# Every engine's order in a graph-attention kernel written out call by call, with the last quarter picked in three pieces

## The chip, the cores and the metric

One core of a Trainium2 chip. The metric is the device time of one execution in microseconds (us), of which 255.73 us is the median of three runs of the kernel before (254.72 to 261.86).

## What is computed

The inputs are x, 4096 x 128, and a dense 4096 x 4096 adjacency matrix in fp32 (64 MB), with few ones. The reference, cut to what matters:

```python
h = jnp.maximum(_layernorm(x, axis=-1), 0.0)
Wh = h @ W
e = leaky_relu((Wh @ a[:d_out])[:, None] + (Wh @ a[d_out:])[None, :], 0.2)
mask = (adj > 0) | jnp.eye(N, dtype=bool)
x = x + softmax(where(mask, e, -9e15), axis=1) @ Wh
h = jnp.maximum(_layernorm(x, axis=-1), 0.0)
x = x + where(adj < 1.0, exp(-(1.0 / adj - 1.0) ** 2 / 0.5), 0.0) @ (h @ W1 + B1)
```

Where every entry of the matrix is 0 or 1, the weights of the last line are all zero, so the kernel computes the attention layer alone and verifies, over the whole matrix, that each entry is 0 or 1. A general path (not run with these inputs) is taken if one is not.

## The kernel before

The matrix is read in 32 **chunks** of 2 MB, two to a **step** (16 steps), eight to a **quarter** of the rows (four quarters, `s` = 0 to 3). SyncE loads chunk i into slot i % 6 of a ring of six, once chunk i - 6 has been used by everyone. For each chunk these pieces of work are issued:

- `check(i)` verifies that its entries are 0 or 1: on ScalarE two passes (L866, L869), or on VectorE one pass (L1035). `DVE_CHECKED` lists the chunks that VectorE takes, all others are ScalarE's.
- `pack(i)` on TensorE turns eight rows' bits and the column number into one word per column in PSUM (L560, L573), and VectorE's `scan(step)` takes the largest words of each segment out of PSUM (L1065) when both chunks of the step are packed.
- `clean_diagonal(i)` and `column(i)` on VectorE, `turn_hub` and `turn_columns` on TensorE, and `hub`/`hub_group` treat the diagonal and the first 128 nodes (the hubs) apart.

A **piece** is a group of steps whose non-zeros are picked together. For piece n the chain is: `pick(n)` (VectorE, rounds of 8 largest), `place(n)` (TensorE), then two branches. The lane branch: `decode(n)` (VectorE) writes `index`. The shared branch: `pick_shared(n)` (VectorE, L1108 to L1131), `place_shared(n)` (TensorE, L646), `decode_shared(n)` (VectorE, L1145 to L1168) writes `shared_index`. GpSimd then issues one indirect DMA for each slot of the group (L478), which gathers rows of a node table in DRAM. When a **group** g has landed, `weigh(g)` (VectorE; L1222 to L1233 for a lane group, to L1239 or L1251 for a shared one) makes weights, and `scatter(g)` (TensorE, L682) adds the group to the accumulators in PSUM. Before, the pieces are the steps 0-3, 4-7, 8-11, 12-14 and 15; they make 11 groups (0 to 10) of 76 indirect DMAs. Groups share a ring of four, so group g is gathered only after group g - 4 has been scattered.

The accumulators of a quarter are begun by `add_columns(s)` (TensorE, L670), get `add_self(s)` (L677, after ScalarE's `scale_self(s)`, L889) and the scatters, and are emptied by `epilogue(s)` (VectorE, L1313 and L1319, eight tiles), after which SyncE stores the quarter. `add_columns(s + 1)` waits for `epilogue(s)`, since both use the same banks. The last quarter ends with `weigh(10)`, `scatter_last` and `last_epilogue` in three parts. `judge()` (VectorE) collects all verdicts of the checks, and `count_bad` (TensorE) must stand before `scatter_last` in TensorE's queue.

Each engine runs its own queue in program order. Before, that order came from a loop over the chunks with tables that say at which chunk a call stands, for instance:

```python
DVE_CHECKED = [0, 1, 4, 2, 5, 7, 10, 12, 14, 17, 19, 21, 31]
SCAN_AT = {2 * n + 2: n for n in range(STEPS - 1)}
PICK_AT = {8: 0, 16: 1, 24: 2, 30: 3}
WEIGH_AT = {13: 0, 15: 1, 17: 2, 20: 3, 22: 4, 25: 5, 28: 6}
EPILOGUE_AT = {19: 0, 27: 1}
```

## Time and profile before

| | |
|---|---|
| Median of 3 runs | 255.73 us (254.72 to 261.86) |
| The profiled execution | 253.61 us, of which the span from first to last instruction is 251.8 us |
| TensorE busy | 170.7 us (68%) |
| VectorE busy | 186.3 us (74%) |
| ScalarE busy | 188.1 us (75%) |
| GpSimd busy | 120.9 us (48%) |
| Mean granted clock of TensorE | 0.846 |
| Moved by DMA | 76.96 MB |

In the rows below, PE is TensorE, DVE VectorE, ACT ScalarE, POOL GpSimd and SP SyncE; PEld is TensorE's weight load. All times are us from the start of the span. In a row of the timeline the numbers are the start and the length, then come engine, line, operation, output<-inputs, count, and in brackets how long the engine sat idle before it and what ended that wait ("remote": no recorded end of an instruction fits the semaphore's change). An end of a matrix multiplication is modelled, so the start of what waited for it is the firmer number.

### The profile page before, as it was taken

Reading aid. Unit: us, or ns where it says so; the run is one execution under the profiler, and the core shown is the slowest. Engines: PE = TensorE matmul, PEld = TensorE weight load, DVE = VectorE, ACT = ScalarE, POOL = GpSimd, SP = SyncE. Lnnn points to the kernel's source line nnn. Section 1 sums busy time; section 2 is a strip of 40 time slices with the busy share of each in tenths; the row PEclk is TensorE's granted clock in tenths of the full one; section 3 lists DMA queues with packets and bytes.
Section 4 is the critical chain, followed back from the end, with each engine's and each line's share of the span. In section 5 each row is a group of like instructions: output and inputs, shape, how many; then the busy total and the mean of one; then the engine's idle time right before and its main releaser. Section 6 shows DMA issues by size and latency. Waiting matters only on the chain. (4 is left out here: it accounts for less than half of the span.)

```text
span 251.8 us, 3251 instructions
## 1 busy us (share of the span) xinstructions
PE 170.7 (68%) x970; PEld 118.5 (47%) x970; DVE 186.3 (74%) x563; ACT 188.1 (75%) x201; POOL 120.9 (48%) x131
## 2 busy tenths in 40 slices
PE   0296797595149849794999787557494929557390
PEld 0295553253135525563576554434353626356390
DVE  7967949989988799999599993865317581067963
ACT  0899876977993089899983999999999999900000
POOL 0395040000007798987689898137760027713810
PEclk9999999979557986999599999797887776965778
DMA  5999999999999999999999999999994001120002
GB/s 160 389 410 411 407 410 415 422 411 408 409 409 405 390 394 395 403 394 395 392 393 401 398 391 397 390 408 389 384 392 187 0 5 40 26 85 0 9 10 90
DMA packets 22389, 76.96 MB, mean 306 GB/s; under 512 B 2643, under 2 KB 3255, under 8 KB 22368
## 3 DMA queue, kind: packets, MB, share of 16 engines
q1 hardware_dynamic: 18912, 71.31, 72.5%
q0 software_dynamic: 3040, 5.34, 6.3%
q8 instruction: 9, 0.15, 0.2%
q10 hardware_dynamic: 416, 0.07, 0.2%
q14 instruction: 12, 0.10, 0.1%
HBM read 74.52 MB, written 4.28 MB: 313 GB/s over the span
## 5 line engine op out<-in xcount | busy, mean ns | idle before, releaser
L478 POOL DMA_INDIRECT gathered_rows<-node_table,index x48 | 68.1, 1418 | 73.2 <-issue 45.2
L573 PE MATMUL bank<-adj_ring,pack_w 128*128 128x512 bf16 (+3 forms) x262 | 73.9, 411 | 5.4 <-DVE clean L1051 2.9
L866 ACT ACTIVATE trash_a<-adj_ring,below_one 128x4096 fp8e4<-128x4096 f32 x19 | 70.4, 3705 | 4.3 <-DMA adj_ring<-in_adj 3.3
L869 ACT ACTIVATE trash_a<-adj_ring 128x4096 fp8e4<-128x4096 f32 x19 | 68.7, 3618 | 0.6
L1035 DVE SCALAR_TENSOR_TENSOR trash_v<-adj_ring 128x4096 fp8e4<-128x4096 f32 x13 | 57.3, 4411 | 0.1
L478 POOL DMA_INDIRECT gathered_rows<-node_table,shared_index x28 | 37.7, 1345 | 17.6 <-DVE shared_index L1156 9.4
L573 PEld LDWEIGHTS bank<-adj_ring,pack_w 128*128 128x128 bf16 x262 | 27.3, 107 | 37.7 <-issue 17.6
L682 PE MATMUL bank<-gathered_rows,spread 128*128 128x129 f32 x176 | 27.3, 321 | 8.9 <-DVE spread L1233 8.6
L1065 DVE MAX8 cand<-bank 128x8 f32<-128x120 f32 (+24 forms) x82 | 23.3, 349 | 11.5 <-PE bank L573 8.0
L682 PEld LDWEIGHTS bank<-gathered_rows,spread 128*128 128x128 f32 x176 | 25.9, 233 | 10.2 <-issue 9.9
L895 ACT ACTIVATE bad_terms<-bank 1x48 f32<-1x48 f32 x1 | 0.2, 200 | 22.7 <-PE bank L699 22.7
L878 ACT ACTIVATE r_rows<-bank 128x512 f32<-128x512 f32 x8 | 4.6, 590 | 16.0 <-remote 11.0
L610 PE MATMUL bank<-whe,hub_w 128*128 128x129 f32 x64 | 10.5, 319 | 7.7 <-DVE hub_w L1272 7.3
L560 PE MATMUL bank<-codes,code_w 128*128 128x512 bf16 x32 | 14.2, 445 | 1.8 <-issue 1.8
L1313 DVE RECIPROCAL rden<-bank 128x3 f32<-128x3 f32 (+1 forms) x12 | 2.0, 168 | 16.6 <-remote 16.5
L610 PEld LDWEIGHTS bank<-whe,hub_w 128*128 128x128 f32 x64 | 9.5, 227 | 9.3 <-DVE hub_w L1272 8.8
L835 ACT ACTIVATE spread<-x_sb,shift,rstd 128x128 f32<-128x128 f32 x32 | 13.3, 502 | 0.0
L670 PE MATMUL bank<-hub_whe,col_w 128*128 128x129 f32 x48 | 7.8, 328 | 7.3 <-DVE x_sb L1319 7.3
L629 PE MATMUL bank<-slots,own_lane 128*32 128x8 f32 (+1 forms) x40 | 2.4, 192 | 14.8 <-issue 13.1
L510 PE MATMUL bank<-w_sb,gathered_rows 128*128 128x130 f32 x64 | 10.5, 315 | 1.3 <-ACT whe L849 1.2
L498 PE MATMUL bank<-ident,spread 128*128 128x128 f32 x32 | 6.5, 338 | 6.8 <-ACT spread L835 6.8
L670 PEld LDWEIGHTS bank<-hub_whe,col_w 128*128 128x128 f32 x48 | 7.2, 238 | 7.9 <-issue 7.9
(165 smaller groups left out, 269.9 us busy)
## 6 DMA issues: line engine op xcount, KB each, us to landing
adj_ring<-in_adj SPq DMA_DIRECT2D x32, 2048.0 KB, 18.1
node_table<-whe POOLq DMA_DIRECT2D x4, 532.0 KB, 10.9
x_sb<-in_x SPq DMA_DIRECT2D x8, 256.0 KB, 6.0
out<-x_sb SPq DMA_DIRECT2D x3, 512.0 KB
gathered_rows<-node_table,index POOLq DMA_INDIRECT x48
gathered_rows<-node_table,shared_index POOLq DMA_INDIRECT x28
out<-x_sb SPq DMA_DIRECT2D x2, 192.0 KB
out<-x_sb SPq DMA_DIRECT2D x1, 128.0 KB
```

The costliest lines, as they stand in the source:

```text
L478: pool.indirect_dma_start(out=rows[:, g % RING_GROUPS * GE + t, :], out_offset=None, in_=table, in_offset=bass.IndirectOffsetOnAxis(ap=row ...
L510: last = nc.tensor.matmul(bank[6 + half][:, b * (D + 2):(b + 1) * (D + 2)], hT[:, nb * P:(nb + 1) * P], w0_sb[:, :], start=(b == 0), stop= ...
L560: nc.tensor.matmul(to[:, :], code_w[:, 2 * c + half, :], codes[:, :], start=True, stop=False, skip_group_check=True)
L573: last = nc.tensor.matmul(to[:, lo:hi], pack_w[:, k, :], ring_hi[:, i % AR, row_at + lo:row_at + hi], start=False, stop=(k == KB - 1), ski ...
L610: last = nc.tensor.matmul(bank[7][:, 0:E1], hub_w[:, m % 2, b, :], whe[:, 4 * HUB_ORDER[m] + b, ONE:ONE + E1], start=(m + b == 0), stop=(m ...
L670: last = nc.tensor.matmul(acc_of(t), weights[:, t, :], hub_whe[:, ONE:ONE + E1], start=(t % 3 == 0), stop=True, skip_group_check=True)
L682: return nc.tensor.matmul(acc_of(t), spread[:, g % 2, t * KB:(t + 1) * KB, :], rows[:, g % RING_GROUPS * GE + turn, ONE:ONE + E1], start=F ...
L835: last = nc.scalar.activation(hn_block(b), x_sb[:, b, :], ACT.Identity, bias=shift[:, b:b + 1], scale=rstd[:, b:b + 1])
L866: nc.scalar.activation(trash_a[:, :], ring[:, i % AR, :], ACT.Sign, bias=below_one[:, :], scale=-1.0, accum_out=signs[:, n:n + 1], saturat ...
L869: nc.scalar.activation(trash_a[:, :], ring[:, i % AR, :], ACT.Abs, accum_out=sizes[:, n:n + 1], saturate=False).then_inc(checked_a, 1)
L1035: nc.vector.scalar_tensor_tensor(trash_v[:, :], ring[:, i % AR, :], 1.0, ring[:, i % AR, :], ALU.is_ge, ALU.not_equal, accum_out=bad_v[:, ...
L1065: last = nc.vector.max(cand[:, at * 8:(at + 1) * 8], word_bank(step, half)[:, lo:hi])
```

## The change

The tables and the loops over the chunks are gone: each engine's calls stand written out in a list. What differs in it:

- Pieces: steps 12 to 14 and 15 become 12 and 13, 14, and 15. Pieces 4 (step 14) and 5 (step 15) have no lane group. There are 12 groups (0 to 11) and 80 indirect DMAs.
- VectorE checks chunks 1, 2, 0, 4, 7, 10, 14, 12, 16, 18, 21, 24 (12 chunks instead of 13, and no chunk after 24); ScalarE checks 20 instead of 19, the last of them in the order 30, 28, 31, 29.
- `shared_index` and `shared_on` have three buffers instead of two; a few waits are added so that the new order is sound (`self_added`, `words_done`).

```diff
 PIECES = [((0, 1, 2, 3), 32, 16, 32), ((4, 5, 6, 7), 24, 16, 16), ((8, 9, 10, 11), 24, 8, 32),
-          ((12, 13, 14), 16, 8, 16), ((15,), 8, 0, 16)]
+          ((12, 13), 16, 8, 16), ((14,), 8, 0, 16), ((15,), 8, 0, 16)]
-DVE_CHECKED = [0, 1, 4, 2, 5, 7, 10, 12, 14, 17, 19, 21, 31]
-ACT_CHECKED = [i for i in range(CHUNKS) if i not in DVE_CHECKED]
+DVE_CHECKED = [1, 2, 0, 4, 7, 10, 14, 12, 16, 18, 21, 24]
+ACT_CHECKED = [3, 5, 6, 8, 9, 11, 13, 15, 17, 19, 20, 22, 23, 25, 26, 27, 30, 28, 31, 29]
-PICK_AT = {8: 0, 16: 1, 24: 2, 30: 3}
-WEIGH_AT = {13: 0, 15: 1, 17: 2, 20: 3, 22: 4, 25: 5, 28: 6}
-        shared_index = sb("shared_index", [P, 2, KB], i32)
+        shared_index = sb("shared_index", [P, 3, KB], i32)
...
@@ the tail of TensorE's list @@
-            add_columns(SG - 1)
+            turn_columns(27)
+            pack(28)
+            add_columns(2)
+            place(3)
+            pack(29)
+            add_self(2)
+            place_shared(3)
+            pack(30)
+            scatter(6)
             place(4)
+            pack(31)
             place_shared(4)
-            add_self(SG - 1)
+            scatter(7)
+            place(5)
+            add_columns(3)
+            place_shared(5)
             scatter(8)
             scatter(9)
+            add_self(3)
+            scatter(10)
             count_bad()
             scatter_last()
@@ of ScalarE's @@
+            row_weights(3, 1)
+            check(25)
+            check(26)
+            check(27)
+            check(30)
+            check(28)
+            check(31)
+            check(29)
             raise_flag()
@@ of VectorE's @@
+            pick(2)
+            clean_diagonal(24)
+            weigh(4)
+            decode(2)
+            pick_shared(2)
+            clean_diagonal(25)
+            decode_shared(2)
+            weigh(5)
+            check(24)
+            column(26)
+            scan(12)
+            scan(13)
+            epilogue(1)
+            column(27)
+            pick(3)
+            pick_shared(3)
+            decode(3)
+            weigh(6)
+            decode_shared(3)
+            scan(14)
+            pick(4)
+            weigh(7)
+            pick_shared(4)
+            scan(15)
+            decode_shared(4)
+            pick(5)
             epilogue(2)
-            scan(STEPS - 1)
-            pick(4)
-            pick_shared(4)
-            decode_shared(4)
-            check(CHUNKS - 1)
+            pick_shared(5)
             weigh(8)
+            decode_shared(5)
             weigh(9)
+            weigh(10)
             judge()
-            weigh(10)
+            weigh(11)
             last_epilogue()
```

Three places show what moves. **VectorE, around the scan of step 15.** Before (L1168 ends `decode_shared(3)`, L1313 and L1319 are `epilogue(2)`, L1065 is `scan(15)`, then `pick(4)`):

```order
L1168 TENSOR_TENSOR shared_on<-stats,std 128x128
L1313 RECIPROCAL rden<-bank 128x3
L1319 SCALAR_TENSOR_TENSOR x_sb<-bank,rden,x_sb 128x128 x3
L1313 RECIPROCAL rden<-bank 128x3
L1319 SCALAR_TENSOR_TENSOR x_sb<-bank,rden,x_sb 128x128 x3
L1313 RECIPROCAL rden<-bank 128x2
L1319 SCALAR_TENSOR_TENSOR x_sb<-bank,rden,x_sb 128x128 x2
L1065 MAX cand<-bank 128x8 x4
L1078 TENSOR_REDUCE full<-cand 128x1
```

Of the change (L1205 ends `pick_shared(4)`, L1137 is `scan(15)`, L1219 to L1242 is `decode_shared(4)`, L1150 begins `pick(5)`):

```order
L1205 TENSOR_SCALAR full<-shared_slots 32x1
L1137 MAX cand<-bank 128x8 x4
L1219 CAST shared_i<-bank 128x4
L1220 TENSOR_SCALAR shared_empty<-bank 128x4
L1222 TENSOR_SCALAR shared_column<-shared_i 128x4
L1224 TENSOR_SCALAR shared_lane<-shared_i 128x4
L1230 TENSOR_TENSOR shared_index<-shared_column,shared_empty 128x4
L1232 TENSOR_TENSOR stats<-shared_i,shared_mask 128x32
L1236 TENSOR_TENSOR std<-shared_lane,lane_number 128x16
L1240 TENSOR_SCALAR stats<-stats 128x32
L1242 TENSOR_TENSOR shared_on<-stats,std 128x128
L1150 TENSOR_REDUCE full<-cand 128x1
```

The scan of step 15 no longer stands behind `epilogue(2)`; the epilogue now follows the pick of step 15.

**VectorE, behind the last `decode_shared`.** Before (L1168 ends `decode_shared(4)`, L1035 is `check(31)`, L1222 begins `weigh(8)`):

```order
L1166 TENSOR_SCALAR stats<-stats 128x32
L1168 TENSOR_TENSOR shared_on<-stats,std 128x128
L1035 SCALAR_TENSOR_TENSOR trash_v,verdicts<-adj_ring 128x4096
L1222 TENSOR_TENSOR edge_w<-r_slots,gathered_rows 128x64
L1225 TENSOR_TENSOR edge_w<-edge_w,gathered_rows 128x64
```

Of the change (L1242 ends `decode_shared(5)`, L1296 begins `weigh(9)`):

```order
L1240 TENSOR_SCALAR stats<-stats 128x32
L1242 TENSOR_TENSOR shared_on<-stats,std 128x128
L1296 TENSOR_TENSOR same<-r_pair,gathered_rows 128x128
L1299 TENSOR_TENSOR same<-same,gathered_rows 128x128
L1302 TENSOR_TENSOR same<-same,shared_on 128x128
```

No check is left on VectorE behind the last index list.

**TensorE, from `add_columns(2)` to the last `pack`.** Before (L670 `add_columns(2)`, L573 x8 `pack(29)`, L682 `scatter(6)`, L629 and L636 `place(3)`, L646 `place_shared(3)`, L560 and L573 x4 `pack(30)`, L677 `add_self(2)`, L682 `scatter(7)`, L573 x8 `pack(31)`):

```order
L573 MATMUL bank<-adj_ring,pack_w 128x512 x8
L682 MATMUL bank<-gathered_rows,spread 128x129 x8
L629 MATMUL bank<-slots,own_lane 32x8 x4
L636 MATMUL bank<-turn_of_p,placed 128x8
L646 MATMUL bank<-half_of_tq,stats 128x4
L560 MATMUL bank<-codes,code_w 128x512
L573 MATMUL bank<-adj_ring,pack_w 128x512 x4
L560 MATMUL bank<-codes,code_w 128x512
L573 MATMUL bank<-adj_ring,pack_w 128x512 x4
L677 MATMUL bank<-whe,ident 128x129 x8
L682 MATMUL bank<-gathered_rows,spread 128x129 x8
L573 MATMUL bank<-adj_ring,pack_w 128x512 x8
```

Of the change (L612 and L619 `place(3)`, L555 x8 `pack(29)`, L660 `add_self(2)`, L629 `place_shared(3)`, L542 and L555 x4 `pack(30)`, L666 `scatter(6)`, L612 `place(4)`, L555 x8 `pack(31)`):

```order
L612 MATMUL bank<-slots,own_lane 32x8 x4
L619 MATMUL bank<-turn_of_p,placed 128x8
L555 MATMUL bank<-adj_ring,pack_w 128x512 x8
L660 MATMUL bank<-whe,ident 128x129 x8
L629 MATMUL bank<-half_of_tq,stats 128x4
L542 MATMUL bank<-codes,code_w 128x512
L555 MATMUL bank<-adj_ring,pack_w 128x512 x4
L542 MATMUL bank<-codes,code_w 128x512
L555 MATMUL bank<-adj_ring,pack_w 128x512 x4
L666 MATMUL bank<-gathered_rows,spread 128x129 x8
L612 MATMUL bank<-slots,own_lane 32x8 x4
L555 MATMUL bank<-adj_ring,pack_w 128x512 x8
```

`place(3)` comes before `pack(29)`, and `scatter(7)` comes behind `pack(31)`.

## Rows read from the trace of the kernel before

**Rows 1.** The page: span, and granted clock and DMA in 40 slices.

```profile
span 251.8 us, 3251 instructions
...
PEclk9999999979557986999599999797887776965778
DMA  5999999999999999999999999999994001120002
```

**Rows 2.** Timeline of SP: the three last chunk loads, and the first store.

```profile
164.67 15.92 SPq L347 DMA_DIRECT2D adj_ring<-in_adj  x3
180.64 42.63 SPq L352 DMA_DIRECT2D out<-x_sb  x3
```

**Rows 3.** Stretches: start:end, length, DVE busy (count), granted clock, DMA share, GB/s.

```profile
153.20:158.00 4.80, 0.00 (x0) 1.00 1.03 395
158.00:171.10 13.10, 10.82 (x49) 0.86 1.03 400
171.10:192.70 21.60, 8.04 (x29) 0.82 0.92 348
192.70:208.60 15.90, 11.84 (x48) 0.71 0.10 38
208.60:220.10 11.50, 0.02 (x1) 0.86 0.16 33
220.10:223.00 2.90, 2.69 (x11) 0.85 0.05 4
```

**Rows 4.** Timeline of DVE, last quarter.

```profile
158.03 0.22 DVE L1222 TENSOR_TENSOR edge_w<-r_slots,gathered_rows 128x64 f32<-128x64 f32 x1 [4.83 <-issue]
...
189.99 0.18 DVE L1313 RECIPROCAL rden<-bank 128x3 f32<-128x3 f32 x1 [4.99 <-remote]
...
220.11 0.18 DVE L1313 RECIPROCAL rden<-bank 128x3 f32<-128x3 f32 x1 [11.49 <-remote]
...
223.01 1.42 DVE L1065 MAX8 cand<-bank 128x8 f32<-128x272 f32 x4
...
229.67 0.16 DVE L1156 TENSOR_TENSOR shared_index<-shared_column,shared_empty 128x4 int32<-128x4 int32 x1
...
230.40 4.42 DVE L1035 SCALAR_TENSOR_TENSOR trash_v<-adj_ring 128x4096 fp8e4<-128x4096 f32 x1
...
242.13 0.29 DVE L1222 TENSOR_TENSOR same<-r_pair,gathered_rows 128x128 f32<-128x128 f32 x1 [2.17 <-DMA gathered_rows<-node_table,shared_index]
```

**Rows 5.** Timeline of PE, from `pack(29)` to `add_columns(3)`.

```profile
196.49 2.81 PE L573 MATMUL bank<-adj_ring,pack_w 128*128 128x512 bf16 x8
...
206.82 0.56 PE L646 MATMUL bank<-half_of_tq,stats 32*128 32x4 f32 x2 [4.13 <-DVE stats L1126]
...
213.51 1.95 PE L682 MATMUL bank<-gathered_rows,spread 128*128 128x129 f32 x16
215.30 1.97 PE L573 MATMUL bank<-adj_ring,pack_w 128*128 128x512 bf16 x8
223.05 3.78 PE L670 MATMUL bank<-hub_whe,col_w 128*128 128x129 f32 x16 [5.79 <-DVE x_sb L1319]
```

**Rows 6.** Timeline of POOL: an undisturbed issue, and the last group's first and last.

```profile
220.23 1.00 POOL L478 DMA_INDIRECT gathered_rows<-node_table,shared_index  x1 [0.30 <-issue]
230.61 5.08 POOL L478 DMA_INDIRECT gathered_rows<-node_table,shared_index  x1 [9.38 <-DVE shared_index L1156]
...
239.31 1.15 POOL L478 DMA_INDIRECT gathered_rows<-node_table,shared_index  x1 [0.30 <-issue]
```

**Rows 7.** Timeline of ACT: its two longest waits, and its last check's second pass.

```profile
87.12 0.60 ACT L878 ACTIVATE r_rows<-bank 128x512 f32<-128x512 f32 x1 [9.46 <-remote]
...
136.34 0.60 ACT L878 ACTIVATE r_rows<-bank 128x512 f32<-128x512 f32 x1 [5.01 <-PE bank L601]
...
213.41 3.71 ACT L866 ACTIVATE trash_a<-adj_ring,below_one 128x4096 fp8e4<-128x4096 f32 x1
...
217.24 3.62 ACT L869 ACTIVATE trash_a<-adj_ring 128x4096 fp8e4<-128x4096 f32 x1
```

More of the change, by code:

```diff
@@ L476, in _ @@
                     at = (g - FIRST_GROUP[n]) * GE + t
-                    row_of = shared_index[:, n % 2, t:t + 1] if IS_SHARED[g] else index[:, n % 3, at:at + 1]
+                    row_of = shared_index[:, n % 3, t:t + 1] if IS_SHARED[g] else index[:, n % 3, at:at + 1]
                     pool.indirect_dma_start(
@@ L760, in _ @@
-            add_columns(SG - 1)
+            pack(0)
+            quad_scores(0)
+            turn_hub(0)
+            pack(1)
+            quad_scores(1)
+            pack(2)
+            pack(3)
+            turn_hub(2)
+            pack(4)
+            hub_group(0)
+            pack(5)
+            hub_group(1)
+            turn_hub(4)
+            pack(6)
+            turn_columns(4)
+            pack(7)
+            hub_group(2)
+            hub_group(3)
+            turn_columns(5)
+            pack(8)
@@ new lines, in _ @@
+            turn_hub(6)
+            place(0)
+            hub_group(4)
+            row_scores(1, 0)
+            pack(9)
+            pack(10)
+            hub_group(5)
+            pack(11)
+            hub_group(6)
+            row_scores(1, 1)
+            place_shared(0)
+            pack(12)
+            pack(13)
+            hub_group(7)
+            add_columns(0)
+            pack(14)
+            add_self(0)
+            turn_columns(14)
+            pack(15)
+            spread_hub()
@@ new lines, in _ @@
+            turn_columns(15)
+            scatter(0)
+            place(1)
+            pack(16)
+            pack(17)
+            place_shared(1)
+            pack(18)
+            scatter(1)
+            pack(19)
+            scatter(2)
+            row_scores(2, 0)
+            row_scores(2, 1)
+            pack(20)
+            add_columns(1)
+            pack(21)
+            turn_columns(20)
+            pack(22)
+            turn_columns(21)
+            pack(23)
+            row_scores(3, 0)
@@ new lines, in _ @@
+            add_self(1)
+            place(2)
+            scatter(3)
+            pack(24)
+            place_shared(2)
+            pack(25)
+            row_scores(3, 1)
+            scatter(4)
+            pack(26)
+            turn_columns(26)
+            pack(27)
+            scatter(5)
+            turn_columns(27)
[7 more added lines that the diff above has]
+            scatter(6)
@@ new lines, in _ @@
+            quad_weights()
+            keep_hub(0)
+            check(3)
+            keep_hub(2)
+            pair_weights()
+            check(5)
+            keep_hub(4)
+            check(6)
+            keep_hub(6)
+            check(8)
+            check(9)
+            row_weights(1, 0)
+            check(11)
+            row_weights(1, 1)
+            scale_self(0)
+            keep_hub_rows()
+            check(13)
+            check(15)
+            check(17)
+            scale_self(1)
@@ L948, in _ @@
+            check(19)
+            row_weights(2, 0)
+            scale_self(2)
+            row_weights(2, 1)
+            check(20)
+            check(22)
+            row_weights(3, 0)
+            check(23)
+            scale_self(3)
+            row_weights(3, 1)
[6 more added lines that the diff above has]
+            check(29)
             raise_flag()
@@ L1073, in pick @@
                     dve.wait_ge(merged, n)
-                    dve.wait_ge(placed_set, n)
+                    dve.wait_ge(placed_set, sum(map(bool, LANE_GROUPS[:n])))
                     dve.wait_ge(full_seen, n)
@@ L1446, in _ @@
-            epilogue(2)
-            scan(STEPS - 1)
-            pick(4)
-            pick_shared(4)
-            decode_shared(4)
-            check(CHUNKS - 1)
+            check(1)
+            quad_masks()
+            check(2)
+            score_terms()
+            check(0)
+            own_and_hub_weights()
+            check(4)
+            scan(0)
+            clear_diagonal(4)
+            hub(0)
+            clean_diagonal(5)
+            scan(1)
+            hub(1)
+            hub(2)
@@ new lines, in _ @@
+            scan(2)
+            hub(3)
+            column(4)
+            clean_diagonal(8)
+            scan(3)
+            hub(4)
+            pick(0)
+            hub(5)
+            decode(0)
+            column(5)
+            clean_diagonal(9)
+            check(7)
+            hub(6)
+            scan(4)
+            hub(7)
+            pick_shared(0)
+            check(10)
+            scan(5)
+            decode_shared(0)
+            weigh(0)
+            check(14)
+            scan(6)
@@ new lines, in _ @@
+            check(12)
+            column(14)
+            scan(7)
+            pick(1)
+            column(15)
+            clean_diagonal(16)
+            weigh(1)
+            clean_diagonal(17)
+            decode(1)
+            pick_shared(1)
+            check(16)
+            weigh(2)
+            decode_shared(1)
+            scan(8)
+            check(18)
+            epilogue(0)
+            scan(9)
+            check(21)
+            column(20)
+            scan(10)
+            column(21)
@@ new lines, in _ @@
+            weigh(3)
+            scan(11)
+            pick(2)
[17 more added lines that the diff above has]
+            decode_shared(3)
```

265 lines of the change are left out of this document (94 added, 171 removed).

## The prediction

> **What bounds the kernel now.** I read the page's slices first. DMA stands at 9 tenths or more from the second slice to the thirtieth and is nearly empty after that [rows 1]. The 32 chunks stream at 395 to 400 GB/s with a DMA share of 1.03, and in the stretch to 192.70 the share is still 0.92; then it is 0.10 [rows 3]. The last load is issued near 180 us [rows 2]. So up to about 190 us the kernel is as fast as its loads, and a change of order can only spoil that part. Behind it stand 62 us (190 to 251.8) in which no chunk arrives: the tail is what the change can shorten.
>
> Next I read who waits in the tail. VectorE does 11.84 us of work in 192.7 to 208.6, then 0.02 us in the 11.5 us up to 220.1 [rows 3]. That hole of 11.49 us is the wait of `epilogue(2)` for `scatter(7)` [rows 4]. Only behind it, at 223.01, comes `scan(15)`, although chunk 31 had landed some 30 us before. TensorE shows the same from its side: it waits 4.13 us with `place_shared(3)` for VectorE and starts `pack(30)` behind that, near 207; `pack(31)` starts at 215.30 [rows 5]. The tail is a sequence of hand-overs between two engines, both mostly idle.
>
> From `scan(15)` to the end the times of before are: 223.01 to the last `shared_index` at 229.67, 6.66 us; to GpSimd's first issue at 230.61, 0.94; to the end of its fourth issue (239.31 + 1.15), 9.85; to the landing at 242.13, 1.67; to the end of the span, 9.67 [rows 4, 6]. Together 28.8 us. One of the four issues takes 5.08 us where an undisturbed one takes 1.00, and it lies exactly beside VectorE's `check(31)` of 4.42 us from 230.40 [rows 4, 6].
>
> **The sum.** I follow the new order from the end of `decode_shared(2)`, 171.10 before.
>
> *Head start.* Before, VectorE stood 4.83 us in front of `weigh(4)` [rows 4], since that call stood ahead of `scan(11)`; all of the stretch from 153.2 to 158.0 is empty [rows 3]. Now `weigh(4)` stands behind `pick(2)`. I take 5 us: `decode_shared(2)` ends at 166. The bounds are 0 (the chunks or ScalarE's `row_weights` hold it anyway) and 7.
>
> *To the end of `epilogue(1)`.* VectorE's work in the stretch that ended with it was 8.04 us [rows 3]. The change adds `check(24)`, 4.42, and puts `scan(13)` ahead of it, 1.42 by the row of `scan(15)` [rows 4]. 166 + 8.04 + 4.42 + 1.42 = 179.9, where it was 192.7. The three loads that were due by then are not late by this: `check(24)` ends near 173.
>
> *To `scan(15)`.* VectorE has 11.84 us less `scan(13)` plus `pick(4)` and `pick_shared(4)` (1.8), about 12. TensorE has more: `add_columns(2)` 3.78, then `place(3)`, `pack(29)`, `add_self(2)`, `place_shared(3)`, `pack(30)`, `scatter(6)`, `place(4)`, `pack(31)`. With 1.95 for eight 129-column fp32 multiplications, 1.97 for a `pack` (2.46 with the two more of an even chunk) and 0.56 for each of the three small ones [rows 5] this is 15.8 us. At half the clock, with 3.78 for the 129-column ones and a `pack` doubled, it is 25.8; the granted clock in these stretches was 0.71 to 0.86 [rows 3]. I take 19, and 2 for the turns in which TensorE waits for `pick_shared(3)` and `pick_shared(4)`. `scan(15)` starts at 201 instead of 223. It cannot come before about 194, by the landing of chunk 31.
>
> *From `scan(15)` to the end.* The scan 1.42; `decode_shared(4)` and `pick(5)` 1.8 (their instructions lie in the 6.66 of before); `epilogue(2)` 2.69; `add_columns(3)` 3.78, ahead of `place_shared(5)` in TensorE's queue; `place_shared(5)` 0.56; 0.4 to the index: 10.7. Then 0.94, four issues of 1.00 + 0.30 = 5.2, landing 1.67, and 9.67: 28.2 us [rows 3 to 6]. So what `check(31)` gives back (9.85 - 5.2 = 4.65) is spent on having `epilogue(2)` and `add_columns(3)` inside this stretch, which is now as long as before.
>
> The indirect DMAs: group 8 waits for the lane index of piece 3, now near 185 where it was 205; twelve issues of 1.3 us are over near 201, so groups 8 and 9 are off the path, as are the four added issues of 5.2 us. The smaller edits (third buffers, added waits) cost nothing: what they wait for lies behind on the same queue or is over.
>
> *Late signals.* `scatter(7)` ends at 213.51 + 1.95 = 215.46 by its row, yet `epilogue(2)`, which waits for nothing else, begins at 220.11: 4.65 us late [rows 4, 5]. The wait of 4.99 us at 189.99 is of this kind. I do not know the cause; both lie beside GpSimd's long runs of issues. The new order has such a run too. I charge it once, 4.6. The bounds are 0 and twice.
>
> The Trainium skill, page "TensorE: Matmul & The Clock Gate", section on the cost of a per-tile semaphore tail, gives some 26 ns for each increment that a matrix multiplication makes. By it no signal would be late, and the sum would be 4.6 us shorter; the rows above say otherwise, and the rows decide.
>
> Span: 201 + 28.2 + 4.6 = 233.8, where it was 251.8. Outside the span the profiled execution had 1.8 us (253.61 - 251.8): 235.6. That execution lay 2.1 under the median of the runs; I add 1.4 for it and predict **237 us**.
>
> **The rivals.**
>
> *ScalarE becomes the bound.* Its last check ended at 217.24 + 3.62 = 220.9, and nobody waited for it. Now it has one check more, 3.71 + 3.62 + some 0.3 = 7.6, and `judge()`, `count_bad` and the last scatters wait for it. For: 228.5 if no idle time is saved, then 0.5 for the verdicts and the same 9.67: span 238.7, time 240.5 to 242. Against: it idled 9.46 and 5.01 us in the middle [rows 7], and its order is rewritten there. With ten of these saved it ends near 218 and the last landing (201 + 4.6 + 18.5 = 224) is later.
>
> *Every hand-over is late* (the other side). The new order has more of them in the tail: `place(3)`, `place_shared(3)`, `scan(14)`, `place(4)`, `scan(15)`, `place_shared(4)`, `epilogue(2)`, `place(5)`, `place_shared(5)`. If eight of nine pay 4.65 as `epilogue(2)` did, it is 37 us: 229.2 + 37 + 1.8 = 268, slower. It decides from 20.8 us on (within 2%: from 16 to 26), that is 2.6 us at each of eight. Against: before, `place_shared(3)` to `decode_shared(3)` and `scan(14)` were prompt, and a lateness that all signals share at one time is paid once when they follow each other.
>
> *A hole in the loads.* `check(24)` moves from ScalarE to VectorE and stands behind `weigh(5)`, which waits for a gather; load 30 waits for it, and `check(7)` and `check(12)` come later than before. A load must be issued before the one ahead has landed, about 180 for load 30. I expect 173. If the lists slip by 7 us and more, each further us is paid in full: 5 us give 242.
>
> *It does not do what it says.* `scan(15)` comes early but the last `shared_index` stays where it is, since `add_columns(3)`, `scatter(7)` and both packs now crowd TensorE at half the clock: 25.8 instead of 19 and as much again behind the scan, +14 us, 251.
>
> **How the numbers follow.** The forecast has 0.68, ScalarE's bound 0.12, a hole in the loads 0.07, no gain 0.06, late hand-overs 0.07 (half of it slower, half of it the same). With the head start at its bounds (+5, -2), TensorE's sum (+7, -3) and the late signals (+4.6, -4.6) not all at one end, the forecast's own range is 230 to 246. To 248 it takes in ScalarE's bound and most holes. A measurement of this kernel tells about 2% from no change (250.6 to 260.8). Faster by more than 2%: 0.87; within: 0.09; slower: 0.04.
>
> **What would show it.** Right: VectorE's `scan(15)` (L1137, the last) near 201 and its hole of 11.5 us gone; GpSimd's last four issues near 1.0 us each, beginning near 213 to 217; `pack(30)` before `pack(31)` with no wait of 4 us; DMA as full as before up to 190. ScalarE's last pass should end at 216 to 222. Wrong would be: DMA below 9 tenths before slice 29, the last pass of ScalarE after 226, or several waits of 3 us and more on VectorE behind TensorE's signals between 185 and 215. The head start is wrong if `epilogue(1)` ends later than 185.

## The result, and the profile after

The changed kernel took **236.5 us** (median of four, 234.53 to 238.15), the kernel before in the same comparison 256.97 (254.72 to 261.86): ratio 0.9205, 95% interval 0.906 to 0.935. The forecast was 237. The profiled execution has a span of 233.5 us at a mean granted clock of 0.880 (forecast 233.8; before 251.8). Some executions of either kernel are a few per cent longer at a lower clock; medians and their ranges take in all executions, ratios and their intervals only the others, so a ratio is not always the quotient of two medians.

From the page of the changed kernel, busy times and the slices:

```profile
PE 164.8 (71%) x982; PEld 117.6 (50%) x996; DVE 186.6 (80%) x591; ACT 195.4 (84%) x205; POOL 129.4 (55%) x135
...
DVE  7984999999199999499992799988999078177972
ACT  0899978999859996999796669999399999999930
...
DMA  5999999999999999999999999999999992003002
```

The loads fill the same stretch as before [rows 1]. VectorE is busy as long as before (186.6 us against 186.3), ScalarE 7.3 us longer and GpSimd 8.5 longer. What went is idle time in the tail.

VectorE's timeline of the changed kernel: start, duration, engine and line, operation, shapes, and in brackets the idle time before it and its releaser. "remote" means that no recorded end of an instruction fits the change that released it:

```profile
165.09 0.42 DVE L1242 TENSOR_TENSOR shared_on<-stats,std 128x256 f32<-128x256 f32 x1
...
178.32 0.16 DVE L1388 RECIPROCAL rden<-bank 128x2 f32<-128x2 f32 x1
...
188.06 0.18 DVE L1182 TENSOR_TENSOR mv<-bank,iota 32x32 f32<-32x32 f32 x1 [7.16 <-remote]
...
200.65 0.18 DVE L1182 TENSOR_TENSOR mv<-bank,iota 32x32 f32<-32x32 f32 x1 [3.05 <-remote]
...
205.69 1.43 DVE L1137 MAX8 cand<-bank 128x8 f32<-128x272 f32 x4 [3.78 <-remote]
...
215.88 0.16 DVE L1230 TENSOR_TENSOR shared_index<-shared_column,shared_empty 128x4 int32<-128x4 int32 x1
...
223.39 0.18 DVE L1411 SCALAR_TENSOR_TENSOR excess<-sizes,signs 128x20 f32<-128x20 f32 x1 [1.23 <-ACT trash_a L909]
```

`decode_shared(2)` ends at 165.5 (171.10 before), `epilogue(1)` near 179.1 (192.7), `scan(15)` starts at 205.69 (223.01), the last `shared_index` is written at 215.9 (229.67 before) [rows 4]. From `scan(15)` to the end of the span are 27.8 us. The hole of 11.49 us in front of `epilogue(2)` is gone, but three waits with "remote" have come: `pick_shared(3)`, `pick_shared(4)`, `scan(15)`. TensorE's timeline of the same kernel:

```profile
181.57 0.39 PE L619 MATMUL bank<-turn_of_p,placed 128*128 128x8 f32 x2
...
183.63 2.14 PE L660 MATMUL bank<-whe,ident 128*128 128x129 f32 x16
190.10 0.58 PE L629 MATMUL bank<-half_of_tq,stats 32*128 32x4 f32 x2 [4.33 <-DVE bits_i L1271]
...
196.87 1.98 PE L555 MATMUL bank<-adj_ring,pack_w 128*128 128x512 bf16 x8
```

`pack(31)` ended at 198.85, and VectorE, idle and waiting for nothing else, began `scan(15)` at 205.69: 6.8 us late. `place(3)` (its last rows are L619) ended near 182 and `pick_shared(3)` began at 188.06, 6.1 late. The ends of multiplications are modelled, but here the queue itself shows that `place(3)` was over: TensorE had gone on to `pack(29)` and `add_self(2)` (L660), done at 185.8. Then it stood 4.33 us in front of `place_shared(3)`, for VectorE's late `pick_shared(3)`. The prediction called this late signals.

GpSimd and ScalarE of the changed kernel:

```profile
168.08 5.24 POOL L460 DMA_INDIRECT gathered_rows<-node_table,index  x1 [0.30 <-issue]
...
190.45 1.00 POOL L460 DMA_INDIRECT gathered_rows<-node_table,index  x1 [4.11 <-DVE index L1262]
...
216.81 0.99 POOL L460 DMA_INDIRECT gathered_rows<-node_table,shared_index  x1 [3.45 <-DVE shared_index L1230]
...
220.74 1.07 POOL L460 DMA_INDIRECT gathered_rows<-node_table,shared_index  x1 [0.30 <-issue]
```

```profile
219.65 3.62 ACT L909 ACTIVATE trash_a<-adj_ring 128x4096 fp8e4<-128x4096 f32 x1
```

The last four issues take 5.0 us (9.85 before [rows 6]); the stretched one now stands beside `check(24)`, at 168.08. ScalarE's last pass ends at 223.3, and `judge` waits 1.23 us for it. So at the end two bounds lie side by side, the last gather and ScalarE.

### The profile page after: what moved, and what is told of

Read it like the earlier page. It is cut to its first block, busy times and chain, and to the rows that moved or that the text cites. A ratio compares the mean times of both kernels' runs of the same rounds, so it can differ in the third digit from the quotient of the medians.

```text
span 233.5 us, 3347 instructions
## 1 busy us (share of the span) xinstructions
PE 164.8 (71%) x982; PEld 117.6 (50%) x996; DVE 186.6 (80%) x591; ACT 195.4 (84%) x205; POOL 129.4 (55%) x135
## 4 chain that ended last, share of the span: by engine, by line
ACT 31%; issue 26%; POOL 13%; DVE 10%; DMA 7%; PE 7%; SPq 2%; another core or an unknown queue 2%; POOLq 0%; DVEq 0%; ACTq 0%
ACT trash_a L906 16%; ACT trash_a L909 13%; POOL gathered_rows L460 13%; DMA adj_ring<-in_adj 7%; DVE trash_v L1106 6%; PE bank L555 3%; ACT whe L946 2%; PE bank L666 2%; SPq L337 2%; PE bank L637 1%; DVE x_sb L1394 1%; DVE spread L1313 1%; PE bank L505 0%; PE bank L584 0%
## 5 line engine op out<-in xcount | busy, mean ns | idle before, releaser
L460 POOL DMA_INDIRECT gathered_rows<-node_table,index x48 | 75.5, 1573 | 49.5 <-issue 42.9
L906 ACT ACTIVATE trash_a<-adj_ring,below_one 128x4096 fp8e4<-128x4096 f32 x20 | 74.1, 3707 | 4.7 <-DMA adj_ring<-in_adj 3.8
L555 PE MATMUL bank<-adj_ring,pack_w 128*128 128x512 bf16 (+3 forms) x255 | 69.6, 402 | 8.9 <-DMA adj_ring<-in_adj 5.1
L909 ACT ACTIVATE trash_a<-adj_ring 128x4096 fp8e4<-128x4096 f32 x20 | 72.3, 3617 | 0.6
L1106 DVE SCALAR_TENSOR_TENSOR trash_v<-adj_ring 128x4096 fp8e4<-128x4096 f32 x12 | 53.0, 4414 | 1.0 <-DMA adj_ring<-in_adj 1.0
L460 POOL DMA_INDIRECT gathered_rows<-node_table,shared_index x32 | 37.6, 1175 | 14.7 <-issue 11.2
L555 PEld LDWEIGHTS bank<-adj_ring,pack_w 128*128 128x128 bf16 x262 | 26.3, 105 | 35.6 <-issue 9.0
L666 PE MATMUL bank<-gathered_rows,spread 128*128 128x129 f32 x192 | 30.4, 324 | 7.0 <-DVE spread L1313 4.6
L666 PEld LDWEIGHTS bank<-gathered_rows,spread 128*128 128x128 f32 x192 | 28.7, 235 | 8.4 <-issue 8.0
L1137 DVE MAX8 cand<-bank 128x8 f32<-128x120 f32 (+24 forms) x82 | 23.2, 351 | 3.8 <-remote 3.8
L946 ACT ACTIVATE whe<-whe,w_self 128x129 f32<-128x129 f32 x32 | 9.8, 389 | 1.9 <-PE bank L593 1.9
L542 PE MATMUL bank<-codes,code_w 128*128 128x512 bf16 x25 | 10.0, 399 | 1.9 <-DMA adj_ring<-in_adj 1.9
L492 PE MATMUL bank<-w_sb,gathered_rows 128*128 128x130 f32 x64 | 10.2, 311 | 1.4 <-ACT whe L889 1.3
L492 PEld LDWEIGHTS bank<-w_sb,gathered_rows 128*128 128x128 f32 x64 | 9.2, 221 | 2.6 <-ACT gathered_rows L881 2.4
L1394 DVE SCALAR_TENSOR_TENSOR x_sb<-bank,rden,x_sb 128x128 f32<-128x128 f32 x32 | 9.4, 345 | 0.4
```

Of the source, the lines that this page charges most:

```text
L460: pool.indirect_dma_start(out=rows[:, g % RING_GROUPS * GE + t, :], out_offset=None, in_=table, in_offset=bass.IndirectOffsetOnAxis(ap=row ...
L492: last = nc.tensor.matmul(bank[6 + half][:, b * (D + 2):(b + 1) * (D + 2)], hT[:, nb * P:(nb + 1) * P], w0_sb[:, :], start=(b == 0), stop= ...
L555: last = nc.tensor.matmul(to[:, lo:hi], pack_w[:, k, :], ring_hi[:, i % AR, row_at + lo:row_at + hi], start=False, stop=(k == KB - 1), ski ...
L666: return nc.tensor.matmul(acc_of(t), spread[:, g % 2, t * KB:(t + 1) * KB, :], rows[:, g % RING_GROUPS * GE + turn, ONE:ONE + E1], start=F ...
L906: nc.scalar.activation(trash_a[:, :], ring[:, i % AR, :], ACT.Sign, bias=below_one[:, :], scale=-1.0, accum_out=signs[:, n:n + 1], saturat ...
L909: nc.scalar.activation(trash_a[:, :], ring[:, i % AR, :], ACT.Abs, accum_out=sizes[:, n:n + 1], saturate=False).then_inc(checked_a, 1)
```

## The experiments

Each study ran on one chip, with the kernel before beside it; the four studies ran on four different chips. Which chip it was turned out to go with a larger difference than most edits made.

### First study: parts of the change

The kernel before took 235.2 us here (233.67 to 237.95, 14 runs), not 256. What these four show holds for a chip on which the kernel before takes that time; the second study has the kernel before at 258. The expectations were all written against 256 and the changed kernel's 236.5, and the changed kernel itself was not run on this chip, so their times cannot be held against these runs as they stand.

**a_head_only**: the old tail behind the new head.

```
-          ((12, 13), 16, 8, 16), ((14,), 8, 0, 16), ((15,), 8, 0, 16)]
+          ((12, 13, 14), 16, 8, 16), ((15,), 8, 0, 16)]
 weigh(5)
-check(24)
-column(26)
-scan(12)
-scan(13)
...
+scan(12)
+column(26)
+epilogue(1)
+scan(13)
...
```

> The new order up to decode_shared(2) and weigh(5) on VectorE (and to the same place on the other engines), behind it the old order, with the old pieces (steps 12 to 14, 15), 11 groups, check(24) on ScalarE and check(31) on VectorE. It prices the head start by itself. Theory of the prediction: decode_shared(2) ends near 166 instead of 171, and all that follows moves by the same 5 us: 251 to 252 against 256.5 of before, scan(15) near 218. Rival, the head start is eaten later (by the loads, which end near 190 in both, or by signals that come late): 255 to 257, scan(15) near 223. Rival, most of the gain is already here: 242 or less.

Measured: 238.6 us, 1.018 of before (1.012 to 1.024). None of the three held: 238.6 lies under the 242 of the last one, but that meant a large gain, and here the kernel is slower than before. The head alone brings nothing on this chip. VectorE waits 8.8 us at 178.2 for ScalarE's `row_weights(3, 1)`, which stands behind `check(24)` and `check(25)`. Its row:

```profile
178.16 0.81 DVE L1357 TENSOR_SCALAR col_w<-r_rows,hub_whe 128x1024 f32<-128x1024 f32 x1 [8.76 <-ACT r_rows L915]
```

**b_check31_act**: one edit in the kernel before.

```
-DVE_CHECKED = [0, 1, 4, 2, 5, 7, 10, 12, 14, 17, 19, 21, 31]
+DVE_CHECKED = [0, 1, 4, 2, 5, 7, 10, 12, 14, 17, 19, 21]
 decode_shared(4)
-check(CHUNKS - 1)
```

> The kernel before with one edit: the pass over chunk 31 is taken from VectorE (behind decode_shared(4)) and given to ScalarE as its last one. Theory of the prediction: GpSimd's four last issues take 5.2 us instead of 9.85, and nobody waits for ScalarE (last pass ends near 228.5, judge comes after it): 4.65 us less, 252. Rival, the issues are slow beside whatever VectorE does: same as before within 1 us. Rival, the late end of ScalarE holds judge and all that stands behind it: 255 or more.

Measured: 237.8 us, 1.015 (1.007 to 1.023): slightly slower; the last rival, ScalarE's late end holds `judge`, is what the trace shows. Up to `decode_shared(4)` it is the program of before on VectorE and GpSimd. VectorE's timeline:

```profile
178.32 0.18 DVE L1313 RECIPROCAL rden<-bank 128x3 f32<-128x3 f32 x1 [0.76 <-PE bank L682]
...
205.04 1.41 DVE L1065 MAX8 cand<-bank 128x8 f32<-128x272 f32 x4
...
209.75 0.16 DVE L1156 TENSOR_TENSOR shared_index<-shared_column,shared_empty 128x4 int32<-128x4 int32 x1
...
223.97 0.18 DVE L1335 SCALAR_TENSOR_TENSOR excess<-sizes,signs 128x20 f32<-128x20 f32 x1 [8.68 <-ACT trash_a L869]
```

`epilogue(1)` starts at 178.3 and not at 189.99, `scan(15)` at 205.0 and not at 223.01 [rows 4], with the same calls in the same order. No wait of VectorE has "remote" in the four traces of this chip. And the last issue ended at 216.2, but `judge` waited 8.7 us for ScalarE's pass over chunk 31: the gathers gained, and ScalarE took the gain and more.

**a_check31_dve**: the same pass, in the changed kernel, back on VectorE.

```
-DVE_CHECKED = [..., 18, 21, 24]
+DVE_CHECKED = [..., 18, 21, 24, 31]
 decode_shared(5)
+check(31)
```

> The changed kernel with the pass over chunk 31 given back to VectorE, behind decode_shared(5); ScalarE has one pass less and ends near 216. Theory 1, the path of the changed kernel runs through group 11's four gathers: one issue is stretched from 1.0 to some 5 us, so 4 to 5 us more, 240.5 to 241.5. Theory 2, ScalarE (last pass ends 223.4, judge waits 1.2 us for it) is as much a bound as the gathers: the same 4 to 5 us more, since the gathers landed at 222.9. Rival, ScalarE alone is the bound at the end: the same time or up to 1 us less.

Measured: 231.3 us, 0.983 (0.978 to 0.989). With ScalarE relieved (its last pass ended at 212.8) the time is low although one issue is stretched. That is nearest to the rival, but it does not settle it, for want of the changed kernel beside it. VectorE's, TensorE's and GpSimd's rows:

```profile
196.08 1.40 DVE L1136 MAX8 cand<-bank 128x8 f32<-128x272 f32 x4
...
206.43 0.16 DVE L1229 TENSOR_TENSOR shared_index<-shared_column,shared_empty 128x4 int32<-128x4 int32 x1
```

```profile
193.40 1.97 PE L555 MATMUL bank<-adj_ring,pack_w 128*128 128x512 bf16 x8 [1.65 <-DMA adj_ring<-in_adj]
```

```profile
207.46 5.21 POOL L460 DMA_INDIRECT gathered_rows<-node_table,shared_index  x1 [0.30 <-issue]
212.97 1.09 POOL L460 DMA_INDIRECT gathered_rows<-node_table,shared_index  x1 [0.30 <-issue]
```

The new order brings `scan(15)` to 196.1 where the old one had 205.0 on the same chip, 9 us, and here `pack(31)` waits for nothing but chunk 31. But the last index comes only 3.3 us earlier (206.4 against 209.8), and the first issue that uses it begins at 212.97, 6.4 us behind it. The stretched issue, still one of the added group 10, makes 4.2 of these; the rest is GpSimd's queue being behind with the twelve gathers of groups 8 and 9 and with group 10.

**a_pieces**: the third piece undone.

```
-          ((12, 13), 16, 8, 16), ((14,), 8, 0, 16), ((15,), 8, 0, 16)]
+          ((12, 13, 14), 16, 8, 16), ((15,), 8, 0, 16)]
 column(27)
+scan(14)
 pick(3)
...
```

> The changed kernel with the old pieces: steps 12 to 14 picked together, then 15, 11 groups, in a new order by hand (scan(14) ahead of pick(3); place(4) and add_columns(3) behind scatter(7)). It prices the third piece. Theory A, the third piece is worth what it costs or more, since group 8's gathers begin before step 14 is scanned: here group 8's first gather comes 3 to 5 us later than 190.45, and the time is 238 to 242. Theory B, the piece is worth nothing, since groups 8 and 9 are off the path and what is saved is work (one pick, one pick_shared, one decode_shared, four gathers, 10 us of GpSimd and VectorE in all): 233 to 237, scan(15) before 203.

Measured: 233.7 us, 0.994 (0.990 to 0.998). Theory B in its numbers: without the piece `scan(15)` starts at 196.9, and the last issue ends at 212.8. What holds the end is ScalarE, so the time does not tell what the third piece is worth:

```profile
220.33 0.18 DVE L1408 SCALAR_TENSOR_TENSOR excess<-sizes,signs 128x20 f32<-128x20 f32 x1 [8.70 <-ACT trash_a L906]
```

### Second study: both kernels again

> The kernel before, unedited, for its trace in this study, since the first four runs stood against 235.2 us and not against 256. Theory C, what cost the 20 us in the profiled execution of before is not in the program: TensorE's signals reach VectorE promptly here (no wait of 3 us and more behind a multiplication that had ended, save the 7 us in front of epilogue(2), where scatter(7) itself is late), index(3) near 192 instead of 205, scan(15) near 205 instead of 223, and the time 234 to 236. Rival, the loads or an engine's own work were slower in the first profile: then the same instructions take longer there, or the DMA share is lower, and this trace shows it.

> The changed kernel, unedited, against the kernel before in this study. Theory C: without late signals only what the program itself gives is left. ScalarE's last pass ended at 223.4 with the late signals and has no idle time that they made (but 4.2 us at 169.5), so the time is 231 to 235, 0 to 2% faster than before, and VectorE's hole in front of pick_shared(3) is 1 to 2 us instead of 7. Rival, the change is worth 18 to 20 us here too: 215 to 218.

On this chip the kernel before took 258.4 us (253.45 to 260.12, 7 runs; b_same 253.3 and 264.5), the changed one 239.3: 0.941 (0.936 to 0.946). So neither the times of Theory C nor its rival held here: this is a chip on which the 20 us are there again. The trace of b_same repeats the first profile, within 0.1 us at both places. VectorE in b_same:

```profile
189.94 0.18 DVE L1313 RECIPROCAL rden<-bank 128x3 f32<-128x3 f32 x1 [4.30 <-remote]
...
220.04 0.18 DVE L1313 RECIPROCAL rden<-bank 128x3 f32<-128x3 f32 x1 [11.52 <-remote]
```

In three of the four studies, and in the first comparison, the median of the kernel before was 256.6 to 260.4 us; in one it was 235.2. It goes with the chip, though each chip was used once, so that something else about the hour is not excluded. What differs in the traces is the waits behind TensorE.

The changed kernel had on this chip four such waits; the fourth, 8.4 us in front of `epilogue(2)`, is behind its longer time, since the last `shared_index` follows it:

```profile
187.29 0.18 DVE L1182 TENSOR_TENSOR mv<-bank,iota 32x32 f32<-32x32 f32 x1 [6.99 <-remote]
...
212.52 0.18 DVE L1388 RECIPROCAL rden<-bank 128x3 f32<-128x3 f32 x1 [8.36 <-remote]
```

**f_check28_dve**: the pass over chunk 28 put into the first of these holes.

```
 pick(3)
+check(28)
...
-check(28)   (ScalarE)
```

> The changed kernel with the pass over chunk 28 moved from ScalarE to VectorE, behind pick(3), where VectorE waited 7.2 us in the profile after. If ScalarE (last pass ends 223.4) is a bound, it now ends 7.6 us earlier and the time falls by 1 to 5 us, to 229 to 233. If VectorE's chain to scan(15) is the bound, the 4.4 us of the pass come on top where no late signal covers them: 235 to 239.

Measured: 238.3 us, 0.934 (0.919 to 0.949), against 0.941 for the changed kernel: 1 us, not told apart. It is the second case of the two expected. ScalarE was idle for 13 us at the end, so it was not the bound on this chip; VectorE still waited 4.4 us in front of `scan(15)` and 4.2 in front of `epilogue(2)`, both with "remote".

### Third and fourth study: why the signals are late

The kernel before took 260.4 (253.83 to 270.62) in the third and 256.6 (255.2 to 268.85) in the fourth. In these three kernels `pick_shared(3)`, `scan(15)` and `epilogue(2)` stand where they stood; only groups 7, 8 and 9 fetch nothing, or other rows, so their results are not the layer's, and the waits for these rows are fitted to it.

```
e_no_gather:    for t in range(0 if g in (7, 8, 9) else ROWS_OF_GROUP[g]):
e_direct_sp:    sp.dma_start(rows[...], table[t * P:(t + 1) * P, :])
e_direct_pool:  pool.dma_start(rows[...], table[t * P:(t + 1) * P, :])
```

> The changed kernel without the twenty indirect DMAs of groups 7, 8 and 9 (what is weighed there are the rows that an earlier group left, so part of the sum is missing). GpSimd is idle from about 176 to 205. It asks why TensorE's signals come late. Theory G, GpSimd's run of issues holds them up: VectorE's waits in front of pick_shared(3), pick_shared(4), scan(15) and epilogue(2), together 15 to 19 us where the kernel before takes 255 and more in this same study, shrink to what TensorE's own work needs, under 1.5 us each, and the time falls to 226 to 233. Theory P, TensorE itself is late (clock, or its own queue): the waits stay, 15 us and more together, 236 to 240. Where the kernel before takes 235 in this study there is nothing late to begin with, and the run tells only what the gathers cost, 0 to 3 us.

> The changed kernel with the twenty indirect DMAs of groups 7, 8 and 9 replaced by twenty plain ones of the same size from the same table, issued by SyncE at the same places (so other rows are weighed than those asked for). Theory G1, the late signals come from GpSimd's issuing: they are gone as without the gathers, 226 to 233. Theory G2, they come from the traffic of small rows, whoever issues it: the waits in front of pick_shared(3), pick_shared(4), scan(15) and epilogue(2) stay at 15 us and more together, 236 to 240.

> The changed kernel unedited once more, beside the two above. Theory C, the size of the gain depends on whether TensorE's signals come late in this study: where the kernel before takes 255 and more, 235 to 240 (ratio 0.91 to 0.95); where the kernel before takes 235, 232 to 235 (ratio 0.985 to 1.0), since ScalarE's last pass ends near 220 to 223 in any case. Rival, the change gives 6 to 8% everywhere: 217 to 221 there.

> The changed kernel with the twenty indirect DMAs of groups 7, 8 and 9 replaced by plain DMAs of the same size, issued by GpSimd at the same places (so other rows are weighed than those asked for). Where the kernel before takes 255 and more: theory G3, it is the writing of descriptors by GpSimd, indirect or not, that holds TensorE's signals up: waits of 3 to 8 us in front of pick_shared(3), scan(15) and epilogue(2) as in the changed kernel, if the plain ones take about 1 us each too; theory G4, only the indirect form does it: waits under 1.6 us, as with SyncE. Where the kernel before takes 235, nothing is late with either.

The unedited kernel, a_same_2: 235.6 us, 0.923 (0.911 to 0.935), as Theory C has it for such a chip. Its VectorE and TensorE:

```profile
187.74 0.18 DVE L1182 TENSOR_TENSOR mv<-bank,iota 32x32 f32<-32x32 f32 x1 [7.28 <-remote]
...
204.62 1.43 DVE L1137 MAX8 cand<-bank 128x8 f32<-128x272 f32 x4 [4.44 <-remote]
...
211.89 0.18 DVE L1388 RECIPROCAL rden<-bank 128x3 f32<-128x3 f32 x1 [4.38 <-remote]
```

```profile
181.12 0.39 PE L619 MATMUL bank<-turn_of_p,placed 128*128 128x8 f32 x2
...
194.94 1.97 PE L555 MATMUL bank<-adj_ring,pack_w 128*128 128x512 bf16 x8
```

`place(3)` ended at 181.5 and `pick_shared(3)` began 6.2 us later; `pack(31)` ended at 196.9 and `scan(15)` began 7.7 us later. Without the gathers, e_no_gather, VectorE and TensorE:

```profile
181.36 0.18 DVE L1183 TENSOR_TENSOR mv<-bank,iota 32x32 f32<-32x32 f32 x1 [1.15 <-PE bank L613]
...
194.38 1.43 DVE L1138 MAX8 cand<-bank 128x8 f32<-128x272 f32 x4 [2.13 <-PE bank L556]
...
222.43 0.18 DVE L1412 SCALAR_TENSOR_TENSOR excess<-sizes,signs 128x20 f32<-128x20 f32 x1 [11.24 <-ACT trash_a L910]
```

```profile
180.88 0.39 PE L620 MATMUL bank<-turn_of_p,placed 128*128 128x8 f32 x2
...
192.37 1.98 PE L556 MATMUL bank<-adj_ring,pack_w 128*128 128x512 bf16 x8 [1.42 <-DMA adj_ring<-in_adj]
```

181.27 to 181.36 and 194.35 to 194.38: both hand-overs are prompt, and no wait of VectorE in the tail has "remote". (One such wait is left, ScalarE's 3.7 us at 168.6, beside the gathers of group 6, which were kept.) Theory G in its mechanism. Its time is wrong: 236.0 us (0.925), no faster than the unedited kernel, for `judge` waits 11.2 us for ScalarE. With plain DMAs from SyncE, e_direct_sp (235.7 us, 0.924; `place(3)` ends at 182.38, `scatter(7)` at 204.49), two hand-overs are prompt; at `scan(15)` VectorE itself was late, waiting for rows:

```profile
182.47 0.18 DVE L1201 TENSOR_TENSOR mv<-bank,iota 32x32 f32<-32x32 f32 x1 [1.15 <-PE bank L625]
...
204.53 0.18 DVE L1407 RECIPROCAL rden<-bank 128x3 f32<-128x3 f32 x1 [1.55 <-PE bank L679]
```

```profile
202.92 0.99 POOL L473 DMA_INDIRECT gathered_rows<-node_table,shared_index  x1 [26.59 <-DVE shared_index L1249]
```

The first came while SyncE was issuing its plain ones (179.0 to 188.4), so, as far as this one hand-over shows, that traffic is not the cause (G1). The second came 1.6 us into a run of four indirect issues by GpSimd: the indirect form alone, without a run of some length, does not make a signal late either. With plain DMAs from GpSimd, e_direct_pool (235.6 us, 0.920), GpSimd, VectorE and TensorE:

```profile
175.96 4.35 POOL L462 DMA_DIRECT2D gathered_rows<-node_table  x8
...
183.98 6.33 POOL L462 DMA_DIRECT2D gathered_rows<-node_table  x12 [3.68 <-DVE index L1267]
```

```profile
195.86 0.18 DVE L1187 TENSOR_TENSOR mv<-bank,iota 32x32 f32<-32x32 f32 x1 [3.21 <-PE bank L617]
...
200.84 1.43 DVE L1142 MAX8 cand<-bank 128x8 f32<-128x272 f32 x4 [3.72 <-PE bank L560]
```

```profile
195.40 0.42 PE L617 MATMUL bank<-slots,own_lane 128*32 128x8 f32 x8
...
197.50 3.30 PE L560 MATMUL bank<-adj_ring,pack_w 128*128 128x512 bf16 x8 [1.68 <-DMA adj_ring<-in_adj]
```

VectorE starts 0.04 us after TensorE ends (195.82 and 200.80), both times; here TensorE itself was late, waiting for chunks. No signal is late. That is G4's picture, but it does not prove G4, for two reasons. A plain DMA took some 0.53 us of GpSimd where an indirect one takes 1.00 and 0.30, so its runs are 4 and 6 us long where those of the indirect ones are 10 and 16. And the plain runs were over (180.3 and 190.3) when these hand-overs came, as was the first at `pick_shared(3)` (182.07). Only `place_shared(3)` to `decode_shared(3)` fell into one: 186.96 to 187.00, 3 us into the second. Whether it is the indirect form or the length of an unbroken run stays open, and so does why one chip of four does not show it.

**g_pieces_check28**: a_pieces with the pass over chunk 28 on VectorE.

```
 column(27)
+check(28)
 scan(14)
...
-check(28)   (ScalarE)
```

> A version meant to beat both kernels: the changed kernel with the old pieces (a_pieces) and the pass over chunk 28 moved from ScalarE to VectorE, ahead of scan(14), where VectorE waited 5.9 us in a_pieces and where the stretched issue of GpSimd falls into a gap of 5 us before group 8. ScalarE, whose last pass held judge for 8.7 us there, ends near 212.5; the last gather landed near 214.5. Theory, GpSimd's queue is the next bound: span 224 to 226, 226 to 228 us where the kernel before takes 235 (ratio 0.96 to 0.97), and 228 to 234 where it takes 255 and more. Rival, the stretched issue pushes all later gathers back by 4 us, so that as much is lost as won: 230 to 235 (or 236 to 240).

Measured, fourth study: 232.4 us, **0.905** (0.899 to 0.912). It is 9.5% below the kernel before. The changed kernel was not run on this chip: elsewhere with late signals it stood at 0.920 to 0.941, the lowest interval from 0.906 on, so that this one is faster is likely and not shown. e_direct_pool, the changed kernel with other rows, stood beside it at 0.920 (0.915 to 0.925). The time fell into the theory's range, but the bound was another. ScalarE's last pass ends at 216.0 and holds nobody. The bound that was expected, GpSimd's queue, is not what holds the end. VectorE and GpSimd:

```profile
199.71 1.43 DVE L1133 MAX8 cand<-bank 128x8 f32<-128x272 f32 x4 [2.22 <-remote]
...
207.69 0.18 DVE L1384 RECIPROCAL rden<-bank 128x3 f32<-128x3 f32 x1 [6.06 <-remote]
```

```profile
180.48 4.77 POOL L460 DMA_INDIRECT gathered_rows<-node_table,shared_index  x1 [0.30 <-issue]
...
215.71 1.00 POOL L460 DMA_INDIRECT gathered_rows<-node_table,shared_index  x1 [8.22 <-DVE shared_index L1226]
```

The pass in the gap cost nothing: behind it VectorE still waited 0.89 us for `pack(29)`, and the stretched issue ended in time for group 8. GpSimd then stood 8.2 us, waiting for an index that hung on `epilogue(2)`, whose signal came 8 us after `scatter(7)` had ended (199.66).

## Why the prediction was right, and where it was right by luck

**What bounds the kernel.** Right: DMA is as full and as long as before. At `epilogue(1)` the new order was 13.6 us ahead, at `scan(15)` 17.3, at the end 18.3. The hand-overs did not become fewer, though: TensorE's wait in front of `place_shared(3)` was to go and is 4.33 us, where it was 4.13.

**Head start, 5 us.** 5.6 measured in the first comparison. The reason given, `weigh(4)` in front of `scan(11)`, explains only part. On the chip without late signals the old order (b_check31_act) ends `decode_shared(2)` at 167.3 and the new one (a_check31_dve) at 165.4, 1.9 us. The rest, 3.7, is likely late signals here too: before, ScalarE stood 9.46 us for one [rows 7], where b_check31_act waited 4.8.

**`epilogue(1)` at 179.9.** Measured 179.1; 179.0 in a_check31_dve. This step stands on VectorE's work alone, and it held on either chip.

**`scan(15)` at 201, and 4.6 for late signals behind it.** Together 205.6; measured 205.69. The sum is right by luck, and its two terms are not: in a_check31_dve, without late signals, `scan(15)` starts at 196.1, and the late signals cost the 9.6 us from there to 205.7, twice the 4.6 that were charged and just beyond their upper bound of 9.2. On one and the same chip, e_no_gather against a_same_2, it is 194.4 against 204.6. TensorE's part was 4 us too long (179.0 to 196.1 is 17.1, not 21). The 19 stood between full and half clock, and its lower end had `add_columns(2)` at 3.78, which is the row at half clock; at full it takes 2.02. In a_check31_dve the granted clock from 179.2 to 196.1 was 1.00, TensorE had its other work done, and `pack(31)` waited for chunk 31 until 193.40: the bound of "about 194" that the prediction named and did not reach. In the profile after, with the late signals, the clock from 179.2 to 193.4 was 0.79.

The prediction's own sign of being wrong was there: several waits of 3 us and more on VectorE behind TensorE between 185 and 215. They are 7.16, 3.05 and 3.78. So by its own test the step with the late signals was off, although the time was right.

The Trainium skill's figure for an increment in a semaphore tail ("TensorE: Matmul & The Clock Gate", section on the cost of a per-tile semaphore tail, some 26 ns) is of the size that the prompt hand-overs show, 0.03 to 0.1 us. Beside GpSimd's indirect issues the traces of three chips of four do not agree with it.

**From `scan(15)` to the end, 28.2.** Measured 27.8, by the steps given: 10.2 to the index (10.7), 5.0 for four issues (5.2). On another chip with late signals (a_same) one fell in this stretch, and the time was 239.3; the first comparison had none there, which was luck too.

**`check(31)` gives 4.65 back.** The four issues shrank by 4.85. That this is won was right only while ScalarE waits behind: on the chip without late signals the move makes the kernel before 1.5% slower, since ScalarE ends at 223.8. And a pass behind the last index stretches an issue wherever GpSimd is just then: in a_check31_dve it was one of group 10.

**ScalarE as a rival, 0.12.** Priced with a last pass at 218 if ten us of idle time were saved, and 228.5 if not; it ended at 223.3, beside the last gather. It was nearer to being the bound than the chance said. e_no_gather and e_direct_sp show it: every late signal removed from the tail, and the time did not move. So the charge of 4.6 did not decide whether the forecast held: with nothing late in the tail ScalarE alone holds the kernel at 236, 1 us from the 237.

**Every hand-over late, 0.07.** The waits with "remote" on VectorE behind 180 sum to 14.0 us (after), 18.4 (a_same) and 17.8 (a_same_2), not to 37: as argued, lateness does not add up over all hand-overs. The three waits of the profile after, 14.0 us, held `scan(15)` up by 9.6.

**What the gain is made of.** The prediction took the hole of 11.49 us and the waits around 180 to 190 for the price of the old order. They were mostly the price of late signals under the old order. The chip without them runs the kernel before in 235 us and not 256, and in b_check31_act `scan(15)` comes at 205.0 with the old order. There the changed kernel itself was not run; its variants, with the pass over chunk 31 back or the third piece undone, stood at 0.983 and 0.994. So what the change is worth, 6 to 8%, is shown where signals are late, and where they are prompt it is likely 2% or less. What part of the gain each edit has where signals are late was not measured: the edits were undone one by one only on the other chip. Had the prediction been asked for that chip, the 18 us that it forecast would have been wrong, and the trace of before had the sign of it: "remote" beside waits whose work had ended.

## What to carry to other kernels

When an engine starts long after the one it waits for has ended, and the profile names no releaser, treat the gap as a cost of its own, apart from the order, and ask whether another chip has it. When an order is packed, an engine that nobody waited for can become the bound, as ScalarE did here: price each taken or given pass on both sides. And put a long VectorE pass where GpSimd's stretched issue ends in a gap of its queue: chunk 28's pass was free there, chunk 31's behind the last index was not.

## What the runs showed of the hardware

- On three of four chips, and in the first comparison, some of TensorE's hand-overs to VectorE came 2 to 10 us late (6.1, 3.7 and 6.8 in the profile after; 9.7 at `epilogue(2)` of a_same) while GpSimd issued indirect DMAs for 10 us and more in a row, or just behind such a run; in the four traces of the fourth chip none did. Four of them came 1.5 to 1.8 us after the end of the run. Not every hand-over in such a run is late: in g_pieces_check28 `pick_shared(3)` followed `place(3)` by 0.5 us. With those twenty DMAs left out, or plain and issued by SyncE or by GpSimd, the hand-overs took 0.03 to 0.1 us, most of those beside GpSimd's plain ones after its runs had ended.
- In a_same_2 the sixteen multiplications of `add_self(2)`, 1.95 us in e_no_gather and 2.14 in the profile after, stretch from 183.40 to 188.53 in such a stretch, so it may be more than the signals that are held up. This stays open.
- An indirect DMA costs GpSimd 1.00 us and 0.30 to the next; a plain one of the same size some 0.53 in all. One beside a check on VectorE (4.42 us) took 4.0 to 5.7, and ended 0.87 us behind the check, whether it had begun before or within it: 235.69 behind 234.82 before, 173.32 behind 172.45 after, 185.25 behind 184.39 in g_pieces_check28.
